# A decoder layer in three stages on one core: batch heads normed in two halves, the last residual tile and the first feed-forward weights loaded earlier

## The chip, the cores and the metric

The kernel runs on one core of one Trainium2 chip. A core has a matrix engine (PE, with its weight loads as PEld), a vector engine (DVE), an activation engine (ACT), GpSimd (POOL) and a queue engine (SP) from which this kernel issues all its transfers; every engine works through its own instructions in order, and semaphores tie them together. The metric is the time of one execution on the device in microseconds, the median of several runs.

## The reference

One layer with three stages for 4 sequences of 1024 tokens of width 512, all in float32:

```python
x = x + mamba_block(layernorm(x))                      # two scans (forward, backward), projection, layer norm
x = x + cross_attention(layernorm(x), ctx, ctx, mask)  # 16 heads of 32, causal, W_q W_k W_v W_o with biases
x = x + expert_attention(layernorm(x))                 # 16 experts, gated q, k, v of width 64, causal, o_proj

def layernorm(x):                                      # eps = 1e-5
    return (x - mean(x, -1)) / sqrt(var(x, -1) + eps)

def mamba_block(x):
    h = x + concat(mamba_f(x), flip(mamba_b(flip(x)))) @ proj_w.T + proj_b
    return layernorm(h) * ln_w + ln_b

def cross_attention(q, k, v, mask):
    s = (q @ W_q.T + b_q) @ (k @ W_k.T + b_k).T / sqrt(32)          # per head
    return softmax(where(causal | mask, -inf, s)) @ (v @ W_v.T + b_v) @ W_o.T + b_o
```

## The kernel before

The program is four blocks one behind the other, with a barrier of all engines between them (`release`): the forward mamba pass (names mf_), the backward pass (mb_), cross-attention (xa_) and the expert attention (ff_). Each block lists its steps once in `order()`; every engine walks that list and does its own part of each step, so the list sets the order of the instructions on all five engines. Nothing is scheduled by costs.

Matrix products are kept exact by splitting both operands in a high and a low part (`matmul3`: three matmuls a product). The high part of a weight or of a transposed tile is made by ACT, the low part by DVE. A tile is 128 tokens by 512 channels.

**Tail of the backward pass.** For tile c (0 to 31) step `output` loads two residual tiles, `partb` (what the forward pass stored) and `xres` (the input), lines 559 and 560. There is one buffer of each, so SP first waits for `out_ready` of tile c-1. ACT norms `xres` to `hb` (L765), POOL adds `partb` (L635), DVE adds the projection (L1027), norms it with a chain of small dependent instructions (L1029 to L1034), POOL multiplies by `lnw`, adds `lnb` and adds `xres` (L637, L639, L641), and SP stores. The buffer `xtok` (two halves by parity of c) holds the tile's tokens; POOL's L613 is its last reader in each tile.

**Heads of cross-attention.** A batch starts with step `head`: `mask` (one row, L1713), `load_x` (1024 tokens to `src`, two transfers of 1 MB), `stats` for eight tiles (L1719), `ln` (L1725, then eleven small dependent instructions in `rsqrt`, L104 to L109, on all eight tiles at once) and `xn` (L1731). Then `src` for n = 0 to 7: PE transposes a tile (L1802), ACT takes the high part (L1640), DVE the low part (L1707). The score banks hold four such tiles, so tile 4 is transposed when the low part of tile 0 is done. Then come the projections `kq` (m = 0 to 7 are q; even m takes the first 512 tokens, odd m the last 512); the first of them waits for all eight low parts. In batch 0 the weights are loaded and split at the head as well (`fetch`, `split`, L1627 and L1695; W_k and W_v go through the same two stage buffers as W_q). For batches 1 to 3 the head is woven into the end of the batch before, whose last four output tiles (`o`, L1885 on PE, residual plus bias L1612 on POOL, sum L1779 on DVE) stand between its parts.

**Head of the feed-forward block.** SP loads tile pair 0 (`load`, L2078), the pair is normed, transposed and split (L2147, L2248), SP loads pair 1 when that is done, and then come the first two of eight weight pieces (`weights`, L2088 on SP, L2135 on ACT, L2222 on DVE), 1 MB each. DVE computes the gate of pair 0 behind the second piece; the first projections (`w`, L72 to L74) fill two banks, and DVE needs the gate to empty them.

Of the kernel before, what the change touches and what calls it, by code (L numbers as in the profile page):

```python
# [15 lines left out]
B = 4  # L16
# [228 lines left out]
def mamba_pass(nc, backward, x_in, w_in, conv_w, conv_b, dt_bias, a_log, d_skip, rms_w, w_out, w_proj,  # L245
# [17 lines left out]
    with ExitStack() as ctx:  # L263
# [236 lines left out]

        def ring(c):
            return (c // GT) % 2, order_t[c % GT]
# [4 lines left out]
        def _(sp):  # L507
# [64 lines left out]
        def _(pool):  # L572
# [53 lines left out]
            def output(c):  # L626
# [8 lines left out]
                g_.tensor_tensor(h, h, partb[:], ALU.add).then_inc(res_ready.sem, 1)  # L635
# [5 lines left out]
                g_.tensor_tensor(h, h, xres[:], ALU.add).then_inc(out_ready.sem, 1)  # L641
# [4 lines left out]
        def _(act):  # L646
# [111 lines left out]
            def output(n):  # L758
                c = n + 2
                if backward and n >= 0:  # L760
                    b, rows = rows_of(n)
                    i = b * NT + rows.start // P
                    wait(act, res_loaded, 2 * n + 1)
                    wait(act, stored[n % 2], n // 2 - 1)
                    a_.activation(hb[:, n % 2, :], xres[:], ACT.Identity, bias=xm[:, i:i + 1], scale=xr[:, i:i + 1])\  # L765
                        .then_inc(xn_ready.sem, 1)
# [499 lines left out]
def cross_attention(nc, x_in, ctx_in, mask_in, wts, bq, bk, bv, bo, out):  # L1266
# [28 lines left out]
    with ExitStack() as ctx:  # L1295
# [69 lines left out]
        dve_step = sig("dve_step", 2 + RSQRT_STEPS)  # L1365
# [84 lines left out]
        def order():  # L1450
# [3 lines left out]
            yield "fetch", 0, 0  # L1454
            yield "fetch", 0, 1
# [3 lines left out]
            for it in range(B):  # L1459
                if it == 0:  # L1460
                    for t in range(NT):
                        yield "xn", 0, t
                    yield "split", 0, 0
# [6 lines left out]
                ahead = list(head()) if it + 1 < B else []  # L1470
                for what, n in ahead[0:2]:
                    yield what, it + 1, n
                for t in range(QT, QT + 2):
                    yield "o", it, t
                for what, n in ahead[2:]:
                    yield what, it + 1, n
                for t in range(QT + 2, NT):
                    if ahead:
                        for i in range(4 * (t - QT - 2), 4 * (t - QT - 2) + 4):
                            yield "xn", it + 1, i  # L1480
                    yield "o", it, t
# [33 lines left out]
        def _(sp):  # L1515
# [11 lines left out]
            def batch(it):  # L1527
# [63 lines left out]
                return {"fetch": fetch, "mask": mask, "load_x": load_x, "load_ctx": load_ctx, "kq": store, "load": load, "scale": move,  # L1591
# [89 lines left out]
        def _(dve):  # L1681
# [16 lines left out]
            def batch(it):  # L1698
# [16 lines left out]
                def stats(t):  # L1715
# [4 lines left out]
                    if t == NT - 1:  # L1720
                        step(last)

                def norm_x(_):
                    for t in range(NT):
                        last = v_.bn_aggr(mv[:, t, :], stat[:, t, :])  # L1725
                    step(last)
                    rsqrt(nc, step, xr[:], mv[:, :, 1], tmp[:, 0, :], tmp[:, 1, :], 1.0, EPS)
# [59 lines left out]
        def _(pe):  # L1787
# [5 lines left out]
            def batch(it):  # L1793
# [11 lines left out]
                def channels(m):  # L1805
# [100 lines left out]
def moe_attention(nc, x_in, wqkv, w_o, sim, gates, out):  # L1906
# [11 lines left out]
    with ExitStack() as ctx:  # L1918
# [59 lines left out]
        def order():  # L1978
# [579 lines left out]
```

## Time and profile before

| what | value |
|---|---|
| median of 3 runs | 4674.73 us (4671.01 to 4688.69) |
| the profiled execution | 4683.56 us, its span 4681.5 us |
| mean granted TensorE clock | 0.950 of full |
| PE, DVE, ACT, POOL busy | 88%, 68%, 35%, 21% |
| mamba passes | start to 2331 us |
| cross-attention | 2331 to 3725 us; batch heads at about 2338, 2684, 3025 and 3363 us |
| feed-forward | 3725 us to the end |

All times in the rows are microseconds from the start of the span. A row of the timeline gives the start, the duration, the engine, the line, the instruction with output and inputs, and in brackets how long the engine had stood idle and what released it. Durations come from one profiled execution, 8.8 us longer than the median.

### The profile page before, as it was taken

How to read it: one execution, taken by the hardware profiler on the slowest of the kernel's cores; microseconds unless marked ns; L12 is line 12 of the kernel's file. 1: busy time of each engine (PE TensorE's matmuls, PEld its weight loads, DVE VectorE, ACT ScalarE, POOL GpSimd, SP SyncE). 2: the span in 40 equal slices, each digit the busy share in tenths (PEclk: the TensorE clock that was granted, in tenths of full speed). 3: DMA queues.
4: the chain of work that ended last, by engine and by line, in shares of the span. 5: the costliest groups of instructions: out<-in, count | busy, mean ns of one | idle time of the engine just before them, and what ended most of it. 6: DMA issues, size and time to landing. Idle time of an engine off the chain costs nothing. (4 is left out here: it accounts for less than half of the span.)

```text
span 4681.5 us, 72445 instructions
## 1 busy us (share of the span) xinstructions
PE 4119.0 (88%) x26392; PEld 3065.9 (65%) x26456; DVE 3185.7 (68%) x6884; ACT 1659.3 (35%) x3487; POOL 1005.7 (21%) x597
## 2 busy tenths in 40 slices
PE   7999999997898898898677887887797789999998
PEld 5777676664665666566366566566576568787787
DVE  5888878874687887888646546546546476666664
ACT  3344333332333333333236536436436321111111
POOL 1333334331244444544500000000000100000000
PEclk8999999998899999999889999999999889999999
DMA  2111001102011011010143143142242120000010
GB/s 101 35 40 40 33 31 38 37 22 99 16 49 42 31 49 42 31 49 31 37 166 96 48 140 87 57 139 77 70 135 68 56 87 31 29 28 28 28 32 19
DMA packets 144917, 265.89 MB, mean 57 GB/s; under 512 B 25140, under 2 KB 31288, under 8 KB 144568
## 3 DMA queue, kind: packets, MB, share of 16 engines
q1 hardware_dynamic: 144568, 261.27, 16.6%
q8 instruction: 215, 3.52, 0.3%
q14 instruction: 134, 1.10, 0.1%
HBM read 164.58 MB, written 88.08 MB: 54 GB/s over the span
## 5 line engine op out<-in xcount | busy, mean ns | idle before, releaser
L1749 DVE TENSOR_REDUCE xa_mn<-xa_s 128x1 f32<-128x896 f32 (+7 forms) x512 | 381.9, 753 | 181.3 <-PE xa_s L1842 155.8
L1665 ACT ACTIVATE xa_src<-xa_s,xa_mn 128x896 f32<-128x896 f32 (+7 forms) x512 | 378.1, 741 | 317.8 <-DVE xa_mn L1749 315.9
L1848 PE MATMUL xa_gen<-xa_ident,xa_src 128*128 128x128 f32 x2304 | 334.9, 283 | 108.7 <-ACT xa_pT L1674 70.7
L1848 PEld LDWEIGHTS xa_gen<-xa_ident,xa_src 128*128 128x128 f32 x2304 | 257.5, 146 | 131.5 <-ACT xa_src L1665 121.4
L72 PE MATMUL ff_wb<-ff_w_hi,ff_st_hi 128*128 128x512 f32 x768 | 321.9, 419 | 16.5 <-DVE ff_parts L2353 10.6
L1612 POOL TENSOR_TENSOR xa_res<-xa_res,xa_bor 128x512 f32<-128x512 f32 x32 | 40.4, 1269 | 1343.7 <-DMA xa_res<-after_mamba_dram 1343.7
L73 PE MATMUL ff_wb<-ff_w_hi,ff_st_lo 128*128 128x512 f32 x768 | 308.7, 402 | 0.0
L74 PE MATMUL ff_wb<-ff_w_lo,ff_st_hi 128*128 128x512 f32 x768 | 308.4, 402 | 0.0
L1203 PE MATMUL mb_ib<-mb_wc,mb_yT 128*128 128x512 f32 x512 | 268.5, 673 | 1.8 <-DVE mb_y L974 1.0
L1757 DVE COPY xa_pT<-xa_gen 128x512 f32<-128x512 f32 (+3 forms) x352 | 186.0, 528 | 108.1 <-PE xa_gen L1848 102.3
L2121 POOL TENSOR_TENSOR ff_mixed<-ff_at,ff_rw 128x1024 f32<-128x1024 f32 x32 | 60.9, 1904 | 876.6 <-DVE ff_at L2381 876.6
L1203 PE MATMUL mf_ib<-mf_wc,mf_yT 128*128 128x512 f32 x512 | 247.4, 629 | 1.8 <-DVE mf_y L974 1.0
L2353 DVE TENSOR_TENSOR ff_parts<-ff_wb,ff_rw 128x512 f32<-128x512 f32 x192 | 132.3, 689 | 150.1 <-PE ff_wb L74 149.4
L848 DVE SCALAR_TENSOR_TENSOR mb_cv<-mb_xc,mb_cw,mb_cv 128x256 f32<-128x256 f32 x432 | 212.8, 529 | 17.3 <-ACT mb_xc L673 16.0
L1674 ACT ACTIVATE xa_pT<-xa_gen 128x512 f32<-128x512 f32 x336 | 188.4, 583 | 89.4 <-PE xa_gen L1848 88.6
L1135 PEld LDWEIGHTS mb_yb<-mb_xdt,mb_decay 128*128 128x128 f32 x1024 | 191.7, 190 | 33.0 <-ACT mb_yT L741 1.4
L848 DVE SCALAR_TENSOR_TENSOR mf_cv<-mf_xc,mf_cw,mf_cv 128x256 f32<-128x256 f32 x432 | 191.4, 480 | 32.2 <-ACT mf_xc L673 31.0
L1135 PEld LDWEIGHTS mf_yb<-mf_xdt,mf_decay 128*128 128x128 f32 x1024 | 191.3, 189 | 31.9 <-ACT mf_yT L741 1.4
L1203 PEld LDWEIGHTS mb_ib<-mb_wc,mb_yT 128*128 128x128 f32 x512 | 104.5, 215 | 132.7 <-issue 132.7
L1864 PE MATMUL xa_acc<-xa_pT,xa_vv 128*32 128x128 f32 x4608 | 155.2, 278 | 37.9 <-DVE xa_pT L1757 15.0
L72 PEld LDWEIGHTS ff_wb<-ff_w_hi,ff_st_hi 128*128 128x128 f32 x768 | 148.1, 193 | 49.7 <-DVE ff_w_lo L2222 16.2
L1203 PEld LDWEIGHTS mf_ib<-mf_wc,mf_yT 128*128 128x128 f32 x512 | 96.3, 198 | 117.6 <-issue 117.6
(511 smaller groups left out, 11405.5 us busy)
## 6 DMA issues: line engine op xcount, KB each, us to landing
xa_qa<-xa_q_dram SPq DMA_DIRECT2D x384, 64.0 KB, 2.0
xa_q_dram<-xa_kq SPq DMA_DIRECT2D x32, 512.0 KB, 2.8
xa_k_dram<-xa_kq SPq DMA_DIRECT2D x32, 512.0 KB, 2.8
xa_ka<-xa_k_dram SPq DMA_DIRECT2D x192, 64.0 KB, 2.0
xa_st<-xa_k_dram SPq DMA_DIRECT2D x192, 64.0 KB, 2.0
mf_xg<-in_x_dram SPq DMA_DIRECT2D x16, 512.0 KB, 5.3
turned_dram<-mf_xt_hi SPq DMA_DIRECT2D x16, 512.0 KB, 2.6
turned_dram<-mf_xt_lo SPq DMA_DIRECT2D x16, 512.0 KB, 4.0
```

Of the source, the lines that this page charges most:

```text
L72: nc.tensor.matmul(out, w_hi, x_hi, start=first, stop=False)
L73: nc.tensor.matmul(out, w_lo, x_hi, start=False, stop=False)
L74: return nc.tensor.matmul(out, w_hi, x_lo, start=False, stop=last)
L848: last = v_.scalar_tensor_tensor(cv[:, m, :], xc[:, m, o:o + GN], cw[:, m, j:j + 1], cv[:, m, :], ALU.mult, ALU.add)
L1135: last = mm(yb["y", c, h // 8][:, h % 8 * HP:(h % 8 + 1) * HP], decay[:, (NQ * c + q) % ER, h % Q4, :], xdt[:, c % 2, h * HP:(h + 1) * HP] ...
L1203: last = mm(ps[:], yT[:, k, :], wc[:, k, :], start=k == 0, stop=k == KI - 1)
L1665: a_.activation(pq[:, hh, 0:w], s1[g, i, hh][:, 0:w], ACT.Exp, scale=-1.0, bias=mn[:, i % 2, hh:hh + 1], accum_out=sums[:, i // QT, i % QT ...
L1674: a_.activation(pT[:, k, 0:w], gen["turn", g, i, k][:, 0:w], ACT.Copy).then_inc(pta_ready.sem, 1)
L1749: v_.tensor_reduce(mn[:, i % 2, hh:hh + 1], s1[g, i, hh][:, 0:(i + 1) * P], AX.X, ALU.min).then_inc(mx_ready.sem, 1)
L1757: v_.tensor_copy(pT[:, k, 0:w], gen["turn", g, i, k][:, 0:w]).then_inc(ptv_ready.sem, 1)
L1848: last = tr(ps[:, n * P:(n + 1) * P], pq[:, hh, j * P:(j + 1) * P], ident[:])
L1864: last = mm(ps[hh * XD:(hh + 1) * XD, c:c + P], vv[:, j, g * HG + hh, :], pT[:, k, a:a + P], start=j == 0, stop=j == i, skip_group_check=True)
```

## The change

Four edits. (1) In the backward pass the residual tiles of the last tile (c = 31) go to the free half of `xtok`, and SP loads them right after those of tile 30. (2) In cross-attention the head norms tiles 0 to 3 and then tiles 4 to 7, each half with its own `rsqrt` chain; the mask row moves behind them, and its load behind `load_x` (in batch 0 behind the first weight load as well). Between batches, output tile 6 stands between the halves and tile 7 behind the mask. (3) The first q (and k) projection waits for the low parts of tiles 0 to 3 only, the second for all. (4) In the feed-forward block weight pieces 0 and 1 are asked for before tile pair 1.

```diff
+        def residual(c):
+            spare = xtok[:, N % 2, :]
+            return (spare[:, 0:D], spare[:, D:2 * D]) if c == N - 1 else (partb[:], xres[:])
...
-                    wait(sp, out_ready, c - 1)
-                    sp.dma_start(partb[:], part[b, rows, :]).then_inc(res_loaded.sem, 16)
-                    sp.dma_start(xres[:], x_in[b, rows, :]).then_inc(res_loaded.sem, 16)
+                    def load_residual(c):
+                        b, rows = rows_of(c)
+                        for t, src in zip(residual(c), (part, x_in)):
+                            sp.dma_start(t, src[b, rows, :]).then_inc(res_loaded.sem, 16)
+                    if c < N - 1:
+                        wait(sp, out_ready, c - 1)
+                        load_residual(c)
+                    if c == N - 2:
+                        wait(sp, base_ready, inner(c))
+                        wait(sp, res_loaded, 2 * c + 1)
+                        load_residual(N - 1)
...
         def head():
+            yield "load_x", 0
+            for half in range(2):
+                for t in range(QT):
+                    yield "stats", half * QT + t
+                yield "ln", half
+                for t in range(QT):
+                    yield "xn", half * QT + t
             yield "mask", 0
-            yield "load_x", 0
-            for t in range(NT):
-                yield "stats", t
-            yield "ln", 0
...
             yield "fetch", 0, 0
+            yield "load_mask", 0, 0
             yield "fetch", 0, 1
...
+                ahead = list(head())
+                cut = ahead.index(("ln", 1)) - QT
+                yield "load_x", it + 1, 0
+                yield "load_mask", it + 1, 0
                 for t in range(QT, QT + 2):
                     yield "o", it, t
-                for what, n in ahead[2:]:
+                for what, n in ahead[1:cut]:
                     yield what, it + 1, n
-                for t in range(QT + 2, NT):
...
+                yield "o", it, QT + 2
+                for what, n in ahead[cut:]:
+                    yield what, it + 1, n
+                yield "o", it, QT + 3
...
                     if m % (2 * NHG) == 0:
                         if it == 0:
                             pe.wait_ge(half_ready, w + 1)
+                        pe.wait_ge(slo_ready.sem, slo_ready.at(it, w * NT + QT - 1))
+                    if m % (2 * NHG) == 1:
                         pe.wait_ge(slo_ready.sem, slo_ready.at(it, (w + 1) * NT - 1))
...
             yield "xT", 0
+            yield "weights", 0
+            yield "weights", 1
             yield "load", 1
             yield "logits", 0
-            yield "weights", 0
-            yield "weights", 1
```

On PE no instruction moves. On DVE, between two batches of cross-attention (xa_res the output tiles, xa_rows the mask row, xa_stat to xa_src the norm, xa_st the low parts), this stands before:

```order
L1779 TENSOR_TENSOR xa_res<-xa_gen,xa_res 128x512 x2
L1713 TENSOR_SCALAR xa_rows<-xa_mask 1x1024
L1779 TENSOR_TENSOR xa_res<-xa_gen,xa_res 128x512 x2
L1719 BN_STATS xa_stat<-xa_src 128x6 x8
L1725 BN_AGGR xa_mv<-xa_stat 128x2 x8
L104 TENSOR_SCALAR xa_tmp<-xa_mv 128x8
...
L1731 TENSOR_SCALAR xa_src<-xa_src,xa_mv,xa_xr 128x512 x4
L1779 TENSOR_TENSOR xa_res<-xa_gen,xa_res 128x512
L1731 TENSOR_SCALAR xa_src<-xa_src,xa_mv,xa_xr 128x512 x4
L1779 TENSOR_TENSOR xa_res<-xa_gen,xa_res 128x512
L1707 TENSOR_TENSOR xa_st<-xa_s,xa_st 128x4x128 x8
```

And now, in the changed kernel (line numbers are its own):

```order
L1800 TENSOR_TENSOR xa_res<-xa_gen,xa_res 128x512 x4
L1739 BN_STATS xa_stat<-xa_src 128x6 x4
L1746 BN_AGGR xa_mv<-xa_stat 128x2 x4
...
L1752 TENSOR_SCALAR xa_src<-xa_src,xa_mv,xa_xr 128x512 x4
L1800 TENSOR_TENSOR xa_res<-xa_gen,xa_res 128x512
L1739 BN_STATS xa_stat<-xa_src 128x6 x4
L1746 BN_AGGR xa_mv<-xa_stat 128x2 x4
L104 TENSOR_SCALAR xa_tmp<-xa_mv 128x4
...
L1752 TENSOR_SCALAR xa_src<-xa_src,xa_mv,xa_xr 128x512 x4
L1733 TENSOR_SCALAR xa_rows<-xa_mask 1x1024
L1800 TENSOR_TENSOR xa_res<-xa_gen,xa_res 128x512
L1727 TENSOR_TENSOR xa_st<-xa_s,xa_st 128x4x128 x8
```

The chain from L104 to L109 (eleven instructions) stands there twice, and the mask row has moved from ahead of the norm to behind it; batch 0 has the same order without the output tiles.

On SP, at the end of the backward pass and the start of cross-attention (xa_vv is the weights' stage buffer), this stands before:

```order
L562 DMA after_mamba_dram<-mb_hb 128x512
L559 DMA mb_partb<-part_dram 128x512
L560 DMA mb_xres<-in_x_dram 128x512
L562 DMA after_mamba_dram<-mb_hb 128x512
...
L1534 DMA xa_src<-after_mamba_dram 128x4x512 x2
L1525 DMA xa_vv<-in_attn_w_dram 128x4x512 x2
L1543 DMA xa_mask<-in_mask_dram 1x1024
```

And now:

```order
L566 DMA mb_xtok<-part_dram 128x512
L566 DMA mb_xtok<-in_x_dram 128x512
L576 DMA after_mamba_dram<-mb_hb 128x512 x2
...
L1554 DMA xa_src<-after_mamba_dram 128x4x512 x2
L1545 DMA xa_vv<-in_attn_w_dram 128x4x512
L1563 DMA xa_mask<-in_mask_dram 1x1024
L1545 DMA xa_vv<-in_attn_w_dram 128x4x512
```

The last residual loads stand ahead of the store of tile 30, and the mask row ahead of the second weight.

On SP, at the start of the feed-forward block (ff_xs is a tile pair, ff_pt and ff_pT the two stage buffers), this stands before:

```order
L2070 DMA ff_simw<-in_ffn_dram 128x4x16
L2071 DMA ff_sgm<-in_ffn_dram 128x16
L2078 DMA ff_xs<-after_attn_dram 128x2x512 x2
L2088 DMA ff_pt<-in_ffn_dram 128x4x512
L2088 DMA ff_pT<-in_ffn_dram 128x4x512
```

And now:

```order
L2093 DMA ff_simw<-in_ffn_dram 128x4x16
L2094 DMA ff_sgm<-in_ffn_dram 128x16
L2101 DMA ff_xs<-after_attn_dram 128x2x512
L2111 DMA ff_pt<-in_ffn_dram 128x4x512
L2111 DMA ff_pT<-in_ffn_dram 128x4x512
L2101 DMA ff_xs<-after_attn_dram 128x2x512
```

The two weight loads no longer stand behind the second pair's load, which has a wait in front of it.

## Rows read from the trace of the kernel before

**Rows 1.** The page: busy time of each engine over the span.

```profile
PE 4119.0 (88%) x26392; PEld 3065.9 (65%) x26456; DVE 3185.7 (68%) x6884; ACT 1659.3 (35%) x3487; POOL 1005.7 (21%) x597
```

**Rows 2.** Timeline, tail of the backward pass: start, duration, engine, line.

```profile
2279.64 2.35 POOL L613 TENSOR_TENSOR mb_y<-mb_y,mb_xtok 128x1024 f32<-128x1024 f32 x1 [0.48 <-DVE mb_y L974]
...
2314.64 1.26 POOL L641 TENSOR_TENSOR mb_hb<-mb_hb,mb_xres 128x512 f32<-128x512 f32 x1
2314.81 1.11 DVE L231 SCALAR_TENSOR_TENSOR mb_ytmp<-mb_ytmp 128x1 f32<-128x1 f32 x1
...
2316.76 0.46 SPq L560 DMA_DIRECT2D mb_xres<-in_x_dram  x1
2320.26 0.81 ACT L765 ACTIVATE mb_hb<-mb_xres,x_m,x_r 128x512 f32<-128x512 f32 x1 [12.49 <-DMA mb_xres<-in_x_dram]
2322.62 0.75 DVE L1027 SCALAR_TENSOR_TENSOR mb_hb<-mb_ib,mb_ry,mb_hb 128x512 f32<-128x512 f32 x1 [5.92 <-POOL mb_hb L635]
```

**Rows 3.** Timeline, head of batch 0 of cross-attention.

```profile
2351.45 1.91 ACT L1627 ACTIVATE xa_wq_hi<-xa_vv 128x2048 fp32r<-128x2048 f32 x1 [30.38 <-DMA xa_vv<-in_attn_w_dram]
2352.25 0.68 DVE L1713 TENSOR_SCALAR xa_rows<-xa_mask 1x1024 fp32r<-1x1024 uint8 x1 [7.47 <-DMA xa_mask<-in_mask_dram]
2352.97 4.84 DVE L1719 BATCH_NORM_STATS2 xa_stat<-xa_src 128x6 f32<-128x512 f32 x8
...
2364.39 2.28 DVE L1695 SCALAR_TENSOR_TENSOR xa_wq_lo<-xa_vv,xa_wq_hi 128x2048 fp32r<-128x2048 f32 x1
...
2372.35 0.47 PE L72 MATMUL xa_gen<-xa_st,xa_wq_hi 128*128 128x512 f32 x1 [1.46 <-issue]
...
2378.86 0.74 DVE L1736 SCALAR_TENSOR_TENSOR xa_kq<-xa_gen,xa_bqc,xa_kq 128x512 fp32r<-128x512 f32 x1
```

**Rows 4.** DMA issues from 2338.0 to 2338.5: transfer, count, size, us to landing.

```profile
xa_src<-after_mamba_dram SPq DMA_DIRECT2D x1, 1024.0 KB, 7.0
```

**Rows 5.** Timeline, between batches 0 and 1 of cross-attention.

```profile
2695.11 0.69 DVE L1779 TENSOR_TENSOR xa_res<-xa_gen,xa_res 128x512 f32<-128x512 f32 x1 [7.93 <-POOL xa_res L1612]
2695.72 4.83 DVE L1719 BATCH_NORM_STATS2 xa_stat<-xa_src 128x6 f32<-128x512 f32 x8
...
2701.26 0.75 DVE L104 TENSOR_SCALAR xa_tmp<-xa_mv 128x8 f32<-128x8 f32 x1
...
2704.07 1.91 DVE L1731 TENSOR_SCALAR xa_src<-xa_src,xa_mv,xa_xr 128x512 f32<-128x512 f32 x4
2704.67 3.67 PE L1802 MATMUL xa_s<-xa_ident,xa_src 128*128 128x128 f32 x16 [8.31 <-DVE xa_src L1731]
...
2708.92 4.87 DVE L1707 TENSOR_TENSOR xa_st<-xa_s,xa_st 128x512 fp32r<-128x512 f32 x8
...
2713.84 0.50 PE L72 MATMUL xa_gen<-xa_st,xa_wq_hi 128*128 128x512 f32 x1 [1.67 <-DVE xa_st L1707]
```

**Rows 6.** Busy time by stretch, same place; PEclk stands before the last two.

```profile
2700.00:2702.00 2.00, 0.00 (x0) 0.00 (x0) 1.93 (x10) 0.00 (x0) 1.26 (x1) 0.92 0.06 20
...
2708.00:2710.00 2.00, 0.60 (x5) 0.28 (x4) 2.00 (x4) 0.72 (x2) 0.00 (x0) 0.88 0.13 48
```

**Rows 7.** Timeline, first q projection of batch 3; nine matmuls, then three, between starts.

```profile
3394.58 0.79 PE L72 MATMUL xa_gen<-xa_st,xa_wq_hi 128*128 128x512 f32 x1 [1.41 <-DVE xa_st L1707]
...
3398.32 0.40 PE L72 MATMUL xa_gen<-xa_st,xa_wq_hi 128*128 128x512 f32 x1
...
3399.02 0.40 PE L72 MATMUL xa_gen<-xa_st,xa_wq_hi 128*128 128x512 f32 x1
```

**Rows 8.** Timeline, head of the feed-forward block.

```profile
3726.69 14.71 SPq L2078 DMA_DIRECT2D ff_xs<-after_attn_dram  x2
...
3741.46 0.46 SPq L2088 DMA_DIRECT2D ff_pt<-in_ffn_dram  x1
...
3747.56 1.91 ACT L2135 ACTIVATE ff_w_hi<-ff_pt 128x2048 fp32r<-128x2048 f32 x1 [5.93 <-DMA ff_pt<-in_ffn_dram]
...
3752.25 2.29 DVE L2222 TENSOR_TENSOR ff_w_lo<-ff_pT,ff_w_hi 128x2048 fp32r<-128x2048 f32 x1 [0.39 <-ACT ff_w_hi L2135]
```

More of the change, by code:

```diff
@@ L634, in output @@
                 wait(pool, xn_ready, c)
-                g_.tensor_tensor(h, h, partb[:], ALU.add).then_inc(res_ready.sem, 1)
+                g_.tensor_tensor(h, h, residual(c)[0], ALU.add).then_inc(res_ready.sem, 1)
                 wait(pool, n_ready, c)
@@ L640, in output @@
                 step.after()
-                g_.tensor_tensor(h, h, xres[:], ALU.add).then_inc(out_ready.sem, 1)
+                g_.tensor_tensor(h, h, residual(c)[1], ALU.add).then_inc(out_ready.sem, 1)
             run({"inputs": inputs, "carry": carry, "output": output})
@@ L764, in output @@
                     wait(act, stored[n % 2], n // 2 - 1)
-                    a_.activation(hb[:, n % 2, :], xres[:], ACT.Identity, bias=xm[:, i:i + 1], scale=xr[:, i:i + 1])\
+                    a_.activation(hb[:, n % 2, :], residual(n)[1], ACT.Identity, bias=xm[:, i:i + 1], scale=xr[:, i:i + 1])\
                         .then_inc(xn_ready.sem, 1)
@@ L1364, in cross_attention @@
         stored = [sig(f"stored{i}", NT // 2, 16) for i in range(2)]
-        dve_step = sig("dve_step", 2 + RSQRT_STEPS)
+        dve_step = sig("dve_step", 2 * (2 + RSQRT_STEPS))
         const_ready, par_loaded, const_dve = sem("const_ready"), sem("par_loaded"), sem("const_dve")
@@ L1460, in order @@
                 if it == 0:
-                    for t in range(NT):
-                        yield "xn", 0, t
                     yield "split", 0, 0
@@ L1469, in order @@
                     yield what, it, n
-                ahead = list(head()) if it + 1 < B else []
-                for what, n in ahead[0:2]:
-                    yield what, it + 1, n
+                if it + 1 == B:
+                    for t in range(QT, NT):
+                        yield "o", it, t
+                    return
+                ahead = list(head())
+                cut = ahead.index(("ln", 1)) - QT
+                yield "load_x", it + 1, 0
+                yield "load_mask", it + 1, 0
                 for t in range(QT, QT + 2):
                     yield "o", it, t
-                for what, n in ahead[2:]:
+                for what, n in ahead[1:cut]:
                     yield what, it + 1, n
-                for t in range(QT + 2, NT):
[L1478 to L1481, printed above, removed]
+                yield "o", it, QT + 2
+                for what, n in ahead[cut:]:
+                    yield what, it + 1, n
+                yield "o", it, QT + 3
         def run(batch):
@@ L1589, in output @@
                     sp.dma_start(out[it, t * P:(t + 1) * P, :], res[:, t % 2, :]).then_inc(stored[t % 2].sem, 16)
-                return {"fetch": fetch, "mask": mask, "load_x": load_x, "load_ctx": load_ctx, "kq": store, "load": load, "scale": move,
+                return {"fetch": fetch, "load_mask": mask, "load_x": load_x, "load_ctx": load_ctx, "kq": store, "load": load, "scale": move,
                      "o": output}
@@ L1719, in stats, with norm_x @@
                     last = v_.bn_stats(stat[:, t, :], src[:, t, :])
-                    if t == NT - 1:
+                    if t % QT == QT - 1:
                         step(last)
-                def norm_x(_):
-                    for t in range(NT):
+                def norm_x(half):
+                    mine = slice(half * QT, (half + 1) * QT)
+                    for t in range(half * QT, (half + 1) * QT):
                         last = v_.bn_aggr(mv[:, t, :], stat[:, t, :])
                     step(last)
-                    rsqrt(nc, step, xr[:], mv[:, :, 1], tmp[:, 0, :], tmp[:, 1, :], 1.0, EPS)
+                    rsqrt(nc, step, xr[:, mine], mv[:, mine, 1], tmp[:, 0, mine], tmp[:, 1, mine], 1.0, EPS)
                 def normed(t):
```

## The prediction

> **What bounds the kernel now.** I read the page first: PE is busy 88% of the span, DVE 68% [rows 1]. The middle of each stage is PE's, and no edit touches it: PE has the same instructions in the same order. What the edits touch are places where PE stands still, so I read the timeline at each of them, all engines together, asking there which wait ends last. There are six: the end of the backward pass, four batch heads of cross-attention, the head of the feed-forward block. At each, the stage behind it starts that much earlier or later, and everything behind moves with it, since barriers or data tie all engines there.
>
> **Tail of the backward pass.** The reader is to see ACT idle for 12.49 us until the last residual lands at 2320.2, and DVE idle 5.92 us behind it [rows 2]. The load could be issued only at 2316.76, when POOL's last instruction on tile 30 (start 2314.64, 1.26 long) had freed the buffer: landing 3.5 us later. Now it goes to half of xtok, whose last reader ends at 2279.64 + 2.35 = 2282.0. SP waits besides for tile 30's own load, which ACT needed a whole tile earlier. So the transfer goes off the path, and next late is POOL, in order: its add for tile 31 starts at 2315.9 instead of 2321.2 and ends at 2317.15; DVE's L1027 could follow at once instead of at 2322.62, which is 5.5 earlier. But DVE has small instructions of its own left. L231 with one element a partition takes 1.11 us beside POOL's L641 [rows 2], ending with it; I expect the same beside the add, which leaves DVE three more of some 0.2 us each to do from 2317.15, so L1027 starts at about 2317.7. I take 4.9 us. Bounds: 5.5 (no such stall) and 3.6 (one more POOL instruction in the way, 1.3).
>
> The Trainium skill ("SBUF — State Buffer", Who interferes with whom) says that a DVE instruction with two SBUF inputs and a GpSimd instruction that reads SBUF exclude each other for the whole instruction. By that rule the trace agrees (1.11 us, to the end of L641), and the gain would be 4.9; without it, 5.5.
>
> **Head of batch 0.** DVE is ready at 2344.8 and idles 7.47 us for the mask row [rows 3], though the first half of x is there at 2338.3 + 7.0 = 2345.3 [rows 4]. With the mask behind the norm DVE starts at 2345.4. Its work, from durations: four stats 2.42, aggregate 0.37, the chain 11 x 0.20 = 2.2, four normed tiles 1.9 (all from [rows 5], halves of eight; 0.20 is the time from the end of L104, 2702.01, to 2704.07 over ten steps; the aggregate is an estimate, the rest of the time between the stats and L104, 0.7 for eight); that is 6.9 a half, 13.8 for both, to 2359.2; mask 0.7; low part of W_q 2.28, to 2362.2 instead of 2366.7, 4.5 earlier (its high part is done at 2353.4, in time). Four low parts at 0.61 end at 2364.6; PE must still transpose tile 7 (0.9), and q starts at 2365.5 instead of 2372.35. But PE fills only three banks, 3 x 2.81 (12 matmuls at 0.234, which is 0.70 for three [rows 7]) to about 2374, and then needs DVE's L1736, which stands behind the low part of W_v. W_v is asked for when W_q's low part ends, so this chain moves by 4.5 only: L1736 ends at 2375.1 instead of 2379.6. Before, PE's fourth projection began at 2372.35 + 8.43 = 2380.8; now at 2375.1. I take 5.7 us; bounds 4.5 (DVE's chain decides alone) and 6.9 (PE's start does). The second weight, now issued behind the mask row, has over 10 us of cover.
>
> **The three heads between batches.** Here I expect a loss. PE idles 8.31 us for the first normed tile [rows 5], which invites halving; but the q projections start only when DVE has done everything, and DVE works without a gap from 2695.72 to 2713.8. What counts is DVE's sum to the point that releases q. Before: 18.1 us. Now: add a second aggregate gap and chain, 2.25; add the mask row, 0.7, which stood ahead of the wait of 7.93 us and was free; subtract four low parts, 2.44; 18.6. Then PE transposes tile 7, 0.9, which was hidden before: 19.5. The x load is issued 0.3 earlier, and so may the output tile be that DVE waits for. Net +1.1 a head. Bounds without the clock: +0.5 (the 0.58 that L104 lost beside POOL [rows 5] goes) and +1.8 (a normed tile is blocked for all of POOL's 1.26 instead).
>
> By the same section of the Trainium skill a tensor_scalar in a two-port mode takes part in that lock. That L104 takes 0.75, where the steps behind it follow each other by 0.20, agrees; which of the two engines starts first there now, I cannot say, hence both bounds.
>
> The clock: PE stopped at 2696.4, the granted clock fell to its low level (1.2 GHz) at about 2701.7, and was at the high one (2.4 GHz) from about 2708.5, 3.8 us after the transposes began [rows 5, 6]. q began at full clock. Now tiles 0 to 3 are transposed from about 2701, tiles 4 to 7 only from 2712.4, behind the low part of tile 0, after over 7 us of idling. I let the clock come back 3.8 us after that, at 2716.2; q starts at 2714.9, so 1.3 us of it run at half rate, a loss of 0.65. Batch 3 pays already: nine matmuls take 3.74 us [rows 7] where 9 x 0.234 is 2.1, a loss of 1.6. So heads 1 and 2 lose 0.65 each, head 3 gains 1.0: +0.3. Bounds: all three at the clock back in time (-1.6), or 4.3 us low from q's start on (2.15 each, +4.9). The three heads together: +3.3 + 0.3 = +3.6, between 0 and +10.
>
> **Feed-forward head.** SP issued the first weights at 3741.46, since the second pair's load stood before them with its wait; ACT then idled 5.93 us, and DVE's low part of piece 1 ended at 3754.5 [rows 8]. Now they are issued right behind the first pair (3726.69), some 14 us earlier, and land long before ACT is free at 3741.63. Two high parts back to back, 3.8, to 3745.4; low parts of 2.29: 3743.5 to 3745.9 and to 3748.1. Everything behind (gate, piece 2, the reuse of the stage buffers) hangs on this chain: 6.4 us. PE's first products start at about 3746, and at their low clock still end before the gate. Bounds: 5 and 7 (pieces 3 to 7 each wait for a transfer of their own, whose latency may vary).
>
> **Sum.** 4.9 + 5.7 - 3.6 + 6.4 = 13.4 us less than the profiled execution, 4683.6 - 13.4 = 4670.2. That execution lies 8.8 above the median of the runs shown, so I predict 4661.3. With all bounds at once: -20 to -2, that is 4655 to 4673 against the median.
>
> **Rivals.** First, the halves pay: if PE rather than DVE set the start of q (for it: its idle 8.31 us; against: DVE's gapless stretch), the second chain and the mask would cost nothing, each head would come 1.8 us early instead of 1.4 late: 4661.3 - 9 = 4652. Second, the loads don't do what they should: the last residual still lands late because SP waits for tile 30's load, or 2 MB of weights right behind it delay the first pair. Both are asked for a whole tile, or ahead of the weights, so that I see at most half of both gains lost: 4661.3 + 5.7 = 4667. Third, slower: the second idle stretch in each of the three heads leaves the clock low well into the projections. If the first four q projections (11.2 us at full clock) ran wholly at half rate, each head would cost 11.2 more, less the 0.65 counted: 4661.3 + 32 = 4693. It decides over the sign when the low clock lasts some 9 us longer a head than I take (13.4 / 3 x 2). Against it: in the three heads shown it was back 3.8 us after work began (batch 1) or 3.7 us after q began (batch 3).
>
> **Numbers.** Chances: forecast 0.69, halves pay 0.12, loads late 0.12, slower 0.04, else 0.03. Half a per cent, 23 us, is about what a measurement can tell from no change here: faster means below 4651.4, slower above 4698.1. Faster gets half of the first rival less a little and a tail of my own case, 0.10; slower 0.02; the same 0.88. The range takes the bounds (4655 to 4673), the first rival, and some us for scatter of three runs that span 17.7: 4649 to 4677.
>
> **What would show it.** ACT's L765 of the last tile starts near 2308, and DVE's L1027 near 2317.7. In batch 0 DVE starts its stats at 2345.4 on the old scale and q starts 6.9 earlier. Between batches PE idles twice, about 5 and 7 us, and from the end of output tile 5 on DVE to the first q matmul it is 19 to 20 us instead of 18.0. In the feed-forward block ACT goes from L2147 straight to the weights. Wrong: a first q matmul between batches that comes less than 18 us after that tile, a clock below full for more than 4 us of q, or an ACT that still waits for weights.

## The result and the profile after

| | before | after |
|---|---|---|
| median, runs side by side | 4686.77 us (7 runs, 4671.01 to 4689.03) | 4658.58 us (7 runs, 4652.02 to 4660.90) |
| profiled execution, span | 4681.5 us | 4657.3 us |
| mean granted clock | 0.950 | 0.952 |

The ratio is 0.9949, 95% interval 0.9934 to 0.9964: 24 us less (17 to 31). The predicted time, 4661.3, was met within 3 us, but not the difference: I had worked out 13.4 us, which is a ratio of 0.9971, outside the interval. The median from which I subtracted, 4674.73, was that of three runs; with four more, the seven runs that the kernel after is compared with had 4686.77, and in the later comparisons 35, 17 and 19 runs of the kernel before had 4679.13, 4684.58 and 4683.73. So it is luck that the time was met: a low base hid that the sum was too small, by 11 us against this measurement and by 6 against a second one below, whose interval still holds the forecast. What follows looks for the missing part.

The page after, busy time of each engine, answers to [rows 1]. DVE has 44 instructions more, eleven for the second chain in each of the four heads, and is busy 7 us longer. PE has the same instructions: 26456 matmuls stand in this trace and 26392 in the one before, where 64 records are missing.

```profile
PE 4139.2 (89%) x26456; PEld 3067.8 (66%) x26456; DVE 3192.9 (69%) x6928; ACT 1657.7 (36%) x3487; POOL 1008.1 (22%) x597
```

**Tail of the backward pass**, timeline after (start, duration, engine, line, as in [rows 2]; the bracket is the idle time and its releaser).

```profile
2310.88 0.81 ACT L779 ACTIVATE mb_hb<-mb_xtok,x_m,x_r 128x512 f32<-128x512 f32 x1
...
2317.85 1.26 POOL L655 TENSOR_TENSOR mb_hb<-mb_hb,mb_xres 128x512 f32<-128x512 f32 x1
2318.01 1.11 DVE L231 SCALAR_TENSOR_TENSOR mb_ytmp<-mb_ytmp 128x1 f32<-128x1 f32 x1
2319.07 1.26 POOL L649 TENSOR_TENSOR mb_hb<-mb_hb,mb_xtok 128x512 f32<-128x512 f32 x1
...
2319.16 1.18 DVE L234 SCALAR_TENSOR_TENSOR mb_ry<-mb_ytmp,mb_ry 128x1 f32<-128x1 f32 x1
...
2320.96 0.75 DVE L1041 SCALAR_TENSOR_TENSOR mb_hb<-mb_ib,mb_ry,mb_hb 128x512 f32<-128x512 f32 x1
```

ACT norms the last tile's residual without a wait, POOL adds it (L649) right behind its add for tile 30 (L655), and DVE's last large instruction (L1027 before, L1041 now) starts 3.11 us after L655 began instead of 7.98: 4.87 gained, 4.9 forecast.

**Head of batch 0**, timeline after, answers to [rows 3].

```profile
2343.16 2.47 DVE L1739 BATCH_NORM_STATS2 xa_stat<-xa_src 128x6 f32<-128x512 f32 x4
...
2357.11 0.68 DVE L1733 TENSOR_SCALAR xa_rows<-xa_mask 1x1024 fp32r<-1x1024 uint8 x1
2357.83 2.29 DVE L1715 SCALAR_TENSOR_TENSOR xa_wq_lo<-xa_vv,xa_wq_hi 128x2048 fp32r<-128x2048 f32 x1
2360.87 3.65 PE L1823 MATMUL xa_s<-xa_ident,xa_src 128*128 128x128 f32 x16 [8.16 <-DVE xa_st L1727]
2364.17 0.78 PE L72 MATMUL xa_gen<-xa_st,xa_wq_hi 128*128 128x512 f32 x1
...
2369.53 1.92 ACT L1647 ACTIVATE xa_wv_hi<-xa_vv 128x2048 fp32r<-128x2048 f32 x1 [2.58 <-DMA xa_vv<-in_attn_w_dram]
...
2374.49 0.50 PE L72 MATMUL xa_gen<-xa_st,xa_wq_hi 128*128 128x512 f32 x1 [0.44 <-DVE xa_kq L1757]
```

The backward pass had ended 1.65 us earlier than before. q starts 8.18 us earlier, 6.5 net, but PE's fourth projection (last line) only 6.31 earlier, 4.7 net (forecast: 5.7): W_v, which sets it, landed 9.0 us after it was asked for, 7.5 before. From DVE's first statistics to q it takes 21.0 us instead of 19.4, so the gain comes from the mask row, which no longer holds DVE up, and not from the halves. The second half of x landed at 2345.91, 0.3 us after the statistics of the first: whether all eight tiles at once, started as early, would do better no run tests.

**Between batches 0 and 1**, timeline after, answers to [rows 5].

```profile
2683.70 0.69 DVE L1800 TENSOR_TENSOR xa_res<-xa_gen,xa_res 128x512 f32<-128x512 f32 x1 [7.42 <-POOL xa_res L1632]
2684.31 2.46 DVE L1739 BATCH_NORM_STATS2 xa_stat<-xa_src 128x6 f32<-128x512 f32 x4
...
2689.24 1.26 POOL L1632 TENSOR_TENSOR xa_res<-xa_res,xa_bor 128x512 f32<-128x512 f32 x1 [2.18 <-DMA xa_res<-after_mamba_dram]
2689.39 2.76 DVE L1752 TENSOR_SCALAR xa_src<-xa_src,xa_mv,xa_xr 128x512 f32<-128x512 f32 x4
2690.84 3.44 PE L1823 MATMUL xa_s<-xa_ident,xa_src 128*128 128x128 f32 x16 [5.06 <-DVE xa_src L1752]
...
2701.03 3.27 DVE L1727 TENSOR_TENSOR xa_st<-xa_s,xa_st 128x512 fp32r<-128x512 f32 x5
2701.85 3.36 PE L1823 MATMUL xa_s<-xa_ident,xa_src 128*128 128x128 f32 x16 [7.57 <-DVE xa_st L1727]
...
2704.97 0.48 PE L72 MATMUL xa_gen<-xa_st,xa_wq_hi 128*128 128x512 f32 x1
```

From the first statistics to q it takes 20.66 us instead of 18.12 (19.5 forecast). Two things make the other 1.2: four normed tiles take 2.76 rather than 1.91, the first of them beside POOL's L1632, and the last four transposes (3.36) run mostly at the low clock (granted clock 0.50 from 2702 to 2704), after two idle stretches of PE. From output tile 3, which the edits don't touch, to q, the three heads take 32.8, 33.0 and 33.5 us instead of 31.1, 30.5 and 32.8: 4.9 lost (3.6 forecast).

**Head of the feed-forward block**, timeline after, answers to [rows 8].

```profile
3708.11 0.51 SPq L2111 DMA_DIRECT2D ff_pT<-in_ffn_dram  x1
...
3722.32 1.90 ACT L2158 ACTIVATE ff_w_hi<-ff_pt 128x2048 fp32r<-128x2048 f32 x1
3724.12 1.90 ACT L2158 ACTIVATE ff_w_hi<-ff_pT 128x2048 fp32r<-128x2048 f32 x1
...
3726.54 2.29 DVE L2245 TENSOR_TENSOR ff_w_lo<-ff_pT,ff_w_hi 128x2048 fp32r<-128x2048 f32 x1
```

The loads are issued as soon as the first pair's, and both weights are there when ACT is free. From the block's first statistics to the end of the second low part: 13.9 us instead of 20.4, so 6.5 gained (6.4 forecast).

**What no step had.** The trace before has a wait of which I had not spoken, in the middle of each batch's projections, in front of the first k matmul:

```profile
2738.02 4.87 DVE L1707 TENSOR_TENSOR xa_st<-xa_s,xa_st 128x512 fp32r<-128x512 f32 x8
2738.85 2.42 PE L1802 MATMUL xa_s<-xa_ident,xa_src 128*128 128x128 f32 x16 [0.51 <-DVE xa_st L1707]
...
2742.94 0.50 PE L72 MATMUL xa_gen<-xa_st,xa_wk_hi 128*128 128x512 f32 x1 [1.67 <-DVE xa_st L1707]
```

and the same place after:

```profile
2729.13 4.86 DVE L1727 TENSOR_TENSOR xa_st<-xa_s,xa_st 128x512 fp32r<-128x512 f32 x8
2729.95 2.42 PE L1823 MATMUL xa_s<-xa_ident,xa_src 128*128 128x128 f32 x16 [0.51 <-DVE xa_st L1727]
...
2732.13 0.48 PE L72 MATMUL xa_gen<-xa_st,xa_wk_hi 128*128 128x512 f32 x1
```

From the last transposes' start to k: 4.09 us before, 2.18 after. The edit that lets q go after four low parts stands in a function that runs for q and for k. I had priced it for q alone.

The two traces compared over the whole span ("heads": from DVE's sum of output tile 3 to q):

| stretch | forecast | the two traces |
|---|---|---|
| mamba passes up to tile 30 (no edit) | 0 | +3.2 |
| tail | -4.9 | -4.9 |
| head of batch 0, to the fourth projection | -5.7 | -4.7 |
| three heads between batches | +3.6 | +4.9 |
| k: four pauses of 1.9, and in batch 3 seven to eight slow matmuls behind one, 1.5 | 0 | -9.2 |
| attention loops, first score to output tile 3, four batches (no edit) | 0 | -8.2 |
| feed-forward head | -6.4 | -6.5 |
| sum; the spans differ by 24.2 | -13.4 | -25.4 |

The 1.2 us between sum and spans are lost, in the main, behind the feed-forward head.

### The profile page after: what moved, and what is told of

It is laid out like the page before. It is cut to its first block and busy times, and to the rows that moved or that the text cites. A ratio compares the mean times of both kernels' runs of the same rounds, so it can differ in the third digit from the quotient of the medians.

```text
span 4657.3 us, 72562 instructions
## 1 busy us (share of the span) xinstructions
PE 4139.2 (89%) x26456; PEld 3067.8 (66%) x26456; DVE 3192.9 (69%) x6928; ACT 1657.7 (36%) x3487; POOL 1008.1 (22%) x597
## 5 line engine op out<-in xcount | busy, mean ns | idle before, releaser
L1632 POOL TENSOR_TENSOR xa_res<-xa_res,xa_bor 128x512 f32<-128x512 f32 x32 | 40.5, 1272 | 1325.9 <-DMA xa_res<-after_mamba_dram 1325.9
L862 DVE SCALAR_TENSOR_TENSOR mb_cv<-mb_xc,mb_cw,mb_cv 128x256 f32<-128x256 f32 x432 | 217.2, 538 | 17.0 <-ACT mb_xc L687 15.7
```

Source lines behind the costliest of these rows:

```text
L862: last = v_.scalar_tensor_tensor(cv[:, m, :], xc[:, m, o:o + GN], cw[:, m, j:j + 1], cv[:, m, :], ALU.mult, ALU.add)
```

## The experiments

Every kernel ran in five rounds beside the kernel before; "-7 us" means what the ratio takes off 4683.

**The kernel before again, and three parts alone.** `same` has no edit. `tail`, `ff` and `xa` have the hunks of the diff above for the residual, for the weights' order, and for all of cross-attention.

> The kernel before, unchanged, profiled a second time: how much of the 24 us between the two profiled executions is chance of one execution. Theory A (the named edits give about 11 us: tail 4.9, first head 4.7, feed-forward head 6.5, less 4.9 for the three heads between batches; the other 11 to 13 us are stretches of low clock inside the attention loops that fall differently from one execution to the next): the ratio is 1.000 within 0.3%, and the distances between the output tiles in the middles of the batches differ from those of the first profile by several us, of either sign. Theory B (the edits cause the gains in the middles of the batches): the middles repeat those of the first profile within 1 us.

Ratio 1.0007 (0.9998 to 1.0016). Of the same instructions this profile spans 4668.6 us, 12.9 less than the first: 6.3 less before cross-attention, 8.1 less in the loops (1041.4 us instead of 1049.5), 3.1 less behind it, and 4.5 more from slow k matmuls in three more batches. So the rows "no edit" of the table are within what one execution differs from another.

> Only the last residual loaded ahead. Both theories: DVE's last large instruction of the backward pass starts 4.9 us earlier relative to tile 30, and the time falls by about 4.9 us (0.1%), if nothing else moves. Theory A: whatever else it shows in the cross-attention is scatter of the clock, up to 10 us of either sign in one profile. Theory B (the gains in the middles come with the cross-attention edits): the middles of the batches are as in the kernel before.

Ratio 0.9993 (0.9983 to 1.0002). From POOL's add of tile 30 to DVE's last large instruction 3.11 us, as in the kernel after: the step itself is exact, its 4.9 us (0.10%) fit the interval, which does not exclude 0.

> Only the feed-forward weights asked for ahead of the second pair. ACT's wait for the first piece (5.93 us) goes; the second piece's low part ends 6.5 us earlier relative to the first statistics; time -6.5 us (0.14%). Cross-attention untouched: theory A allows its middles to differ by several us all the same, theory B does not.

Ratio 0.9985 (0.9976 to 0.9995): -7 us. First statistics to second low part: 13.9 us, as after.

> Only the cross-attention edits: halves in all four heads, mask behind, first q released by four low parts. Theory A: first head -4.7, heads between batches +1.7, +2.4 and +0.7, together about 0 against the kernel before, apart from the chance of the clock in the middles (some us either way in a profile, smaller in the median). Theory B: the middles of the batches are shorter by about 18 us in sum here too, so -18 us (ratio 0.996).

Ratio 0.9993 (0.9983 to 1.0002). The traces say that this kernel should gain 4.7 + 9.2 - 4.9, about 9 us, and the median says 3, the interval ending at 8. Its loops took 1045.2 us, its three heads 33.5 each, and there is no pause ahead of k in any batch. B's 18 us are excluded. A's zero is inside, but A had no k in it, so this median does not speak for what k is worth; the 9 us lie just outside. `same`, whose program is the kernel before, came out 3 us above it in this comparison.

**Rebuilding after, and taking its parts apart.**

> The kernel after once more, instruction for instruction. The three single edits gave ratios of 0.9993 (tail), 0.9985 (feed-forward) and 0.9993 (cross-attention), in sum 0.9971 or -13.6 us. Theory A (the parts add up, the rest of the 28 us between the first two medians was the draw of seven runs): 0.997, about 4665 against 4679. Theory B (together the edits give more than apart): 0.995 again, below 4660.

Ratio 0.9960 (0.9946 to 0.9973), 4662.50 us. With the first measurement (0.9949) that is -19 and -24 us. The three parts alone add up to 0.9971, whose uncertainty (some 0.16%) reaches 0.9955. This decides neither for A nor for B.

`norel`: the first projection waits for all again.

```diff
-                        pe.wait_ge(slo_ready.sem, slo_ready.at(it, w * NT + QT - 1))
-                    if m % (2 * NHG) == 1:
                         pe.wait_ge(slo_ready.sem, slo_ready.at(it, (w + 1) * NT - 1))
```

> The kernel after, but the first q matmul waits again for all eight low parts of the normed tiles instead of four. My theory: four low parts of 0.61 us stand between the release and PE: q starts 2.4 us later less the 0.9 of tile 7's transpose, which then lies beside them, so 1.5 us a head in four heads, and less in batch 0, where the projections wait for DVE at their fourth anyway: +5 us, 0.1%. Rival (DVE's low parts compete with other work and q starts no earlier for the release): 0.

4677.28 us, ratio 0.9986 (0.9977 to 0.9996): 15 us slower than the kernel after in the same comparison, three times what I expected. In the profiles q starts 1.5 to 2.4 us later in each of four heads, 7.5 in all, where I expected 5. More lies between q and the first score, 11.2 us in this pair of profiles: 48.4, 46.9, 50.0 and 48.4 us in the four batches, against 46.6, 44.9, 46.0 and 44.9. That is where I found k's pause.

`krel` undoes the rest instead: the kernel before, and only k's release changed.

```diff
-                        pe.wait_ge(slo_ready.sem, slo_ready.at(it, (w + 1) * NT - 1))
+                        pe.wait_ge(slo_ready.sem, slo_ready.at(it, w * NT + QT - 1 if w == 1 else (w + 1) * NT - 1))
+                    if m % (2 * NHG) == 1 and w == 1:
+                        pe.wait_ge(slo_ready.sem, slo_ready.at(it, (w + 1) * NT - 1))
```

> The kernel before with one change: the k projections start when four of the eight low parts of the context are there, not eight (q waits for eight as before). New theory: in every trace with the old wait PE stands still for 1.67 to 1.72 us in front of the first k matmul of each batch, and in 11 of 20 such places 7 or 8 of the k matmuls behind it run at 0.63 us instead of 0.40; with the wait on four it never stands still. So 1.9 us a batch and 0.8 more on average for the clock: 4 x 2.7 = -11 us, ratio 0.9977; from the first q matmul to the first k matmul 27.2 instead of 29.1 us. Rival (PE only shifts its wait to the second k product, which needs the other four low parts): the distance to the first score's minimum stays 46.9, ratio 1.000.

4666.54 us, ratio 0.9968 (0.9956 to 0.9980): -15 us, 9 to 21, for this one wait. Timeline of its batch 1, same place:

```profile
2731.77 4.86 DVE L1707 TENSOR_TENSOR xa_st<-xa_s,xa_st 128x512 fp32r<-128x512 f32 x8
...
2732.60 2.42 PE L1802 MATMUL xa_s<-xa_ident,xa_src 128*128 128x128 f32 x16 [0.51 <-DVE xa_st L1707]
...
2734.78 0.48 PE L72 MATMUL xa_gen<-xa_st,xa_wk_hi 128*128 128x512 f32 x1
```

In all four batches the first k matmul comes 27.2 us after the first q matmul, and the first score's minimum 45.0 us after it; in the kernel before they are 29.1 and 46.9 or more. The rival (a wait only shifted) is out. By the traces this wait is the largest single part of the change.

`nok` is the kernel after without it.

```diff
-                        pe.wait_ge(slo_ready.sem, slo_ready.at(it, w * NT + QT - 1))
+                        pe.wait_ge(slo_ready.sem, slo_ready.at(it, w * NT + QT - 1 if w == 0 else (w + 1) * NT - 1))
```

> The kernel after, but k waits for all eight low parts of the context again (q keeps its release by four). New theory: 4 x 2.7 = 11 us slower than the kernel after, about 4672 on the scale on which the kernel after had 4662.5 and the one before 4684.6 (ratio to before 0.9972), which is what my prediction, that had only q's release, should have met. Rival (the surplus of the kernel after is the chance of the clock in the attention loops): 0.9955, as after.

4663.39 us, ratio 0.9964 (0.9950 to 0.9977). The theory said 0.9972, the rival 0.9955, and both lie inside. In its trace the pauses are back (1.72, 1.67, 1.67, 1.67), and from q to the first score the four batches take 190.6 us, 8.2 more than in `full`; but no slow k matmuls follow in any of the four, and its loops took 1033.6 us, next to the least of all profiles, so that its span (4656.1 us) is shorter than that of the kernel after. A miss as a proof: the pause is in the trace, its price in the median of six runs is not (2 us against `full`, with an uncertainty of about 9). All profiles together give a better price than the medians: from q to the first score the four batches take 192.6 us in the mean of the seven profiles with the pause and 182.4 in the seven without, so k is worth about 10 us, 7.8 of it the pauses and the rest slow matmuls behind them.

`xa0` has only batch 0 in halves, with the mask row behind, and the old release of q and k.

> Only batch 0's head in halves with the mask row behind, no release by four. From the traces with and without the release: DVE starts 7.6 us earlier, and from its first statistics to q it takes 22.8 instead of 19.4, so q starts 4.2 us earlier and the second weight behind it does not delay it: -4, ratio 0.999, not to be told from 1.000 by much. Rival (batch 0 stays bound by DVE's low part of W_v at the fourth projection): -4 at q, but less at the first score, -2 or less.

4679.82 us, ratio 0.9991 (0.9983 to 1.0000): -4 us. q starts 6.21 us earlier than in the first profile of before and 0.09 earlier than in its second; counted from the start of the span, the scatter ahead of cross-attention (6.3 us) hides the step. Counted from DVE's last large instruction of the backward pass it is there: q comes 45.2 us behind it, against 49.7 and 49.6 in the two profiles of before, 4.5 earlier where I expected 4.2. From q to the first score it is 48.2 us, 1.3 more than the 46.9 of before, and that looks like the rival. It is not: PE has no idle time at the fourth projection, and the first six q matmuls take 0.63 to 0.77 us instead of 0.40 to 0.47, which makes the 1.3. The median cannot tell -4 from -2.

**Are halves right between batches?** `rel` keeps all of the kernel after but there: one norm of eight tiles, and the mask row ahead of it again.

```diff
-                ahead = list(head("halves"))
-                cut = ahead.index(("ln", 1)) - QT
+                ahead = list(head("whole"))
+                yield "load_mask", it + 1, 0
                 yield "load_x", it + 1, 0
-                yield "load_mask", it + 1, 0
+                yield "mask", it + 1, 0
                 for t in range(QT, QT + 2):
                     yield "o", it, t
-                for what, n in ahead[:cut]:
+                for what, n in ahead[:NT + 1]:
+                    yield what, it + 1, n
+                for what, n in ahead[NT + 1:NT + 1 + QT]:
                     yield what, it + 1, n
                 yield "o", it, QT + 2
-                for what, n in ahead[cut:]:
+                for what, n in ahead[NT + 1 + QT:]:
                     yield what, it + 1, n
-                yield "mask", it + 1, 0
                 yield "o", it, QT + 3
```

> As the kernel after, but between batches the order of before (mask row ahead of the wait for the output tile, one chain for all eight tiles), with the first q still released by four low parts instead of eight. My theory (halves between batches cost 1.2 us of a second chain, 0.7 of the mask row and 0.9 of the late transpose of tile 7, and the early release gives 2.4 back): from the first statistics to q 18.0 - 2.4 + at most 0.9 (tile 7 on PE is already done) = 15.7 us instead of 20.7, and from output tile 3 to q some 3 to 4 us less than after in each of three heads: -10 us against the kernel after. Rival (the halves pay, since PE starts on its transposes earlier and its clock is back sooner): from output tile 3 to q no less than after, the clock low for the first q matmuls in all three heads, and no gain.

4651.98 us, ratio 0.9933 (0.9919 to 0.9946): 10.5 us less than the kernel after in the same comparison. From output tile 3 to q the heads take 30.0, 29.1 and 29.9 us, against 33.4, 33.4 and 33.1: 10.9 in three heads. Timeline of the head between batches 0 and 1:

```profile
2683.65 4.83 DVE L1746 BATCH_NORM_STATS2 xa_stat<-xa_src 128x6 f32<-128x512 f32 x8
...
2692.39 3.68 PE L1830 MATMUL xa_s<-xa_ident,xa_src 128*128 128x128 f32 x16 [7.95 <-DVE xa_src L1759]
...
2697.47 3.65 PE L1830 MATMUL xa_s<-xa_ident,xa_src 128*128 128x128 f32 x16 [1.41 <-DVE xa_st L1734]
...
2700.77 0.78 PE L72 MATMUL xa_gen<-xa_st,xa_wq_hi 128*128 128x512 f32 x1
```

17.1 us from the statistics to q, not 15.7: I had taken PE to be done with tile 7, but its buffer for tiles 4 to 7 comes free with DVE's low part 0, and four transposes at the low clock take 3.65. Even so the rival (halves pay for themselves) is out: together with the mask row's new place they cost 3.6 us a head.

`early` moves the eight statistics between output tiles 4 and 5, into the wait for output tile 5's residual, where DVE stood idle 7.4 to 7.9 us (what was expected of `early` and `early2` calls it tile 4's).

```diff
-                for t in range(QT, QT + 2):
-                    yield "o", it, t
-                for what, n in ahead[:NT + 1]:
+                yield "o", it, QT
+                for what, n in ahead[:NT]:
                     yield what, it + 1, n
-                for what, n in ahead[NT + 1:NT + 1 + QT]:
+                yield "o", it, QT + 1
+                for what, n in ahead[NT:NT + 1 + QT]:
```

> As rel, but DVE does the eight statistics of the next batch while it waits for the residual of output tile 4 (7.4 to 7.9 us of idling), and only then its output tile 5. My theory: the x halves land some 6 and 8.5 us after they are issued behind output tile 3's residual, so that the statistics end about as output tile 5's residual comes; of the 18 us from the first statistics to q 4.8 go from DVE's chain, less what output tile 5 is late: another 3 to 5 us a head less than rel, -10 to -15 in all, about 4640 to 4645. Rival (the residual and the x loads share the queues, or the clock is low at q because PE has idled as long and starts earlier): output tile 5 is late by as much as the statistics were early, 0 to 2 us a head.

4639.66 us, ratio 0.9910 (0.9896 to 0.9925): 12 us less than `rel` by the medians. From output tile 3 to q 26.7, 27.0 and 26.7 us, 8.6 less than `rel` in three heads. Timeline of the same head:

```profile
2676.41 2.47 DVE L1746 BATCH_NORM_STATS2 xa_stat<-xa_src 128x6 f32<-128x512 f32 x4 [2.56 <-DMA xa_src<-after_mamba_dram]
...
2679.32 2.48 DVE L1746 BATCH_NORM_STATS2 xa_stat<-xa_src 128x6 f32<-128x512 f32 x4 [0.44 <-DMA xa_src<-after_mamba_dram]
...
2681.82 0.69 DVE L1807 TENSOR_TENSOR xa_res<-xa_gen,xa_res 128x512 f32<-128x512 f32 x1
...
2683.29 1.26 POOL L1638 TENSOR_TENSOR xa_res<-xa_res,xa_bor 128x512 f32<-128x512 f32 x1 [2.01 <-DMA xa_res<-after_mamba_dram]
2683.30 1.27 DVE L105 TENSOR_SCALAR xa_xr<-xa_tmp 128x8 int32<-128x8 int32 x1
...
2693.05 3.39 PE L1830 MATMUL xa_s<-xa_ident,xa_src 128*128 128x128 f32 x16 [2.57 <-DVE xa_st L1734]
...
2696.09 0.78 PE L72 MATMUL xa_gen<-xa_st,xa_wq_hi 128*128 128x512 f32 x1
```

The statistics end 0.5 us after POOL's addition for output tile 5, so that this tile is hardly late. PE still idles 2.57 us for low part 0 of DVE; `early2` shortens that.

```diff
...
+                yield "od", it, QT + 1
+                for what, n in ahead[NT:NT + 1 + QT]:
+                    yield what, it + 1, n
+                for t in range(QT):
+                    yield "xn", it + 1, QT + t
+                    yield "lo", it + 1, t
+                yield "od", it, QT + 2
+                yield "od", it, QT + 3
...
```

("od" and "lo" are DVE's parts of output tile and of source tile, now orders of their own.)

> As the kernel with the statistics during the wait for output tile 4's residual (4639.7 against 4684.6), with DVE's work between batches interleaved further: behind the first four normed tiles a normed tile and a low part in turn, and output tiles 6 and 7 only behind the fourth low part. My theory: PE can transpose tile 4 when low part 0 is done, some 2.5 us earlier than now, so it idles 1 us instead of 2.6, and q starts 1.6 us earlier a head: another -5 us, about 0.990. Rival (the release of q needs low part 3, which moves back behind four normed tiles, and output tiles 6 and 7 hold the banks that the projections need): 0 to +3 us.

4632.58 us, ratio 0.9898 (0.9882 to 0.9914), 26 us less than the kernel after had in its own comparison: the fastest of all. Statistics to q 17.65 us instead of 19.68, timeline:

```profile
2692.21 0.68 DVE L1744 TENSOR_TENSOR xa_st<-xa_s,xa_st 128x512 fp32r<-128x512 f32 x1
2692.81 0.54 DVE L1769 TENSOR_SCALAR xa_src<-xa_src,xa_mv,xa_xr 128x512 f32<-128x512 f32 x1
2693.03 0.63 PE L1840 MATMUL xa_s<-xa_ident,xa_src 128*128 128x128 f32 x4 [0.42 <-DVE xa_st L1744]
...
2695.74 0.47 PE L72 MATMUL xa_gen<-xa_st,xa_wq_hi 128*128 128x512 f32 x1
```

PE now waits 0.4 us for each low part in turn, and its clock is at the high level when q starts (0.47, not 0.78). Against `early` the medians are from different comparisons; by the ratios it is 6 us, with an uncertainty of about 10, and by the traces 5.2 in three heads.

## Why the prediction was right, and where it was not

**Tail: right, in size and mechanism.** What keeps the gain at 4.87 rather than 5.5 is the stall that I expected beside POOL's add for tile 31 (L649, 2319.07 to 2320.33). It hit L234, which started at 2319.16, took 1.18 us instead of 0.16 and ended at 2320.34, with three small instructions still to come. The stall of L231 at 2318.01 stands in the trace before as well. The Trainium skill ("SBUF — State Buffer", Who interferes with whom) says that a DVE instruction with two SBUF inputs contends with a GpSimd instruction that reads SBUF; the trace agrees.

**Head of batch 0: right mechanism, 1.0 us too large.** q itself started 6.5 us earlier, the fourth projection, which decides, only 4.7, since it hangs on W_v. I let that chain move with W_q's low part and gave the transfer its old latency; it took 1.5 us longer. That goes with q's early release and not with the halves: the transfer took 8.7 to 9.0 us in the seven profiles in which q is released by four low parts, and 7.4 to 7.5 in the other seven, `xa0` and `norel` with their halves among them. Why is open; the same loads stand right behind it in both.

**Heads between batches: sign right, 3.6 forecast, 4.9 in the traces.** The step that halving costs DVE's sum was right, and `rel` shows it directly. Its size was off by the blocked normed tile (0.85) and by the transposes: I had only tile 7's (0.9) behind four low parts, but all of tiles 4 to 7 wait for low part 0, and at the low clock it takes 3.9 us from there to q where I had 3.3. The start of the statistics came earlier by 0.5 to 1.9, where I had 0.3. My fear for the clock, 0.65 us in two heads, did not come: q's matmuls were at the high level from the start in heads 1 and 2.

**The early release: a step that was missing.** The prediction said "subtract four low parts, 2.44", once a head, for q. The text on the change even said "the first q (and k) projection". So k's wait was put at nothing, without a reason. It was visible (1.67 at 2742.94), is executed four times, and in 14 of the 28 profiled batches with it the matmuls behind ran slow. With the other steps at their traced sizes (4.9, 4.7, -4.9 and 6.5, together 11.2) and about 10 us for k the sum is 21; measured were 24 (17 to 31) and 19 (13 to 25). The medians of `xa` and `nok`, which alone would give k less, are the evidence against it.

**Feed-forward head: right**, 6.5 and 6.4.

**Rivals.** "Halves pay" (4652) had about the difference that came out, for the wrong reason: undoing the halves made the kernel faster. "Loads late" and "slower by the clock" did not occur.

**What stays open.** The 8.2 us in the loops are as much as identical kernels differ by (1049.5 and 1041.4 before, 1041.3 and 1047.1 after); over 14 profiles they run from 1033.3 to 1050.5. It is where the granted clock is at its low level that makes this: in the four loops together that is 10 us in `nok` and `early2` and 58 to 61 in the first profile of before, `rel` and `early`, and over the 56 single loops each microsecond at the low level goes with 0.33 more of loop, the rest scattering by 0.3 us. The edits do not show in it: the loops take 1042.3 us in the mean of the seven profiles with k's pause and 1043.2 in the seven without. What sets where the low level falls is open, and so is why `xa` gained less and `krel` (15 us, 9 to 21) more than their traces say.

## What to carry to other kernels

A wait that is edited inside a function counts at every place where the function runs: list these places and read each one's idle time in the trace. Before halving a chain, see which engine ends last: here it was DVE, which does the chain, and not PE, which waits for its first half, so that the second chain was paid for in full; DVE's idle time (7.4 us a head) was worth 9 us in three heads when work was moved into it. And take the base of a difference from runs beside the changed kernel, since three runs of the old one lay 4 to 12 us off.

## What was not expected of the hardware

Behind a pause of TensorE as short as 1.67 us the matmuls can run slow for a while. Timeline of `same`, k's start in batch 1:

```profile
2736.49 0.67 PE L72 MATMUL xa_gen<-xa_st,xa_wk_hi 128*128 128x512 f32 x1 [1.67 <-DVE xa_st L1707]
2736.96 0.63 PE L73 MATMUL xa_gen<-xa_st,xa_wk_lo 128*128 128x512 f32 x1
```

Seven or eight k matmuls take 0.63 us where others take 0.40. The granted clock was 1.00 up to 2736, through the transposes and into the pause, 0.50 from 2737 to 2740, and 1.00 again from 2741. Seven profiles with the pause show it in 14 of 28 batches, seven without it in 0 of 28. It is not regular: `same` has it in all four batches, the first profile of the same program in one, `nok` in none.

A DVE instruction on 128x8 elements, 0.17 us otherwise, took 1.27 in `early` (L105, 2683.30), as long as POOL's addition beside it, which began at 2683.29 and ended at 2684.55.
